# A transformer block on one core: merged narrow diagonal steps, a ring of five exponentials, a written-out order, and the maxima's splitting on GpSimd

## What is computed

```
x = x + 0.5 * ffn(layernorm(x), W_gate, W_qkv)      # layer 0
x = x + attn(layernorm(x), gamma, beta, W_in, ...)  # the branch: gates, a scan over time, W_out, W_skip
x = x + 0.5 * ffn(layernorm(x), W_gate, W_qkv)      # layer 1
```

```
gating = softmax(x @ W_gate.T); pick the top head h of each row
q, k, v = split(x @ W_qkv.T);  k_shared = k[h];  v_shared = v[h] * gating[h]
att = softmax(causal(q_head @ k_shared.T / 4));  y_head = att @ v_shared
```

## Time and profile before

| | |
|---|---|
| median of three runs | 886.76 us |
| span of the profiled execution, which is its own time | 889.9 us |
| busy: TensorE, VectorE, ScalarE, GpSimd | 844.8, 747.1, 720.6, 295.7 us |
| mean granted TensorE clock | 0.974 of full speed |
| exponentials on ScalarE | 802, mean 767 ns |
| masks on GpSimd | 256, mean 411 ns |

### The profile page before, as it was taken

One profiled execution on the slowest core, in us unless ns is written; L12 is line 12 of the kernel. 1 busy time (PEld: TensorE's weight loads), 2 busy tenths in 40 slices (PEclk: granted clock), 3 DMA queues, 4 the chain that ended last, 5 costly groups with the idle time before them and its releaser, 6 DMA issues.

```text
span 889.9 us, 19042 instructions
## 1 busy us (share of the span) xinstructions
PE 844.8 (95%) x6460; PEld 291.6 (33%) x6460; DVE 747.1 (84%) x2379; ACT 720.6 (81%) x1169; POOL 295.7 (33%) x568
## 2 busy tenths in 40 slices
PE   9898999999999999999999999999999999999997
PEld 6433423332222332324233433342223323222221
DVE  5898778999999989887945889999998999999920
ACT  1148677868998788888979887889998788999996
POOL 3225404633104415046355445632113424110110
PEclk9899689999999999999999999999999999999999
DMA  6110000110000000100010002000001000000000
GB/s 189 49 43 19 2 2 5 57 43 20 1 2 2 1 1 1 43 18 3 1 53 9 2 2 61 3 1 26 1 1 39 25 25 3 24 3 1 2 1 24
DMA packets 20256, 18.03 MB, mean 20 GB/s; under 512 B 4144, under 2 KB 20160, under 8 KB 20160
## 3 DMA queue, kind: packets, MB, share of 16 engines
q1 hardware_dynamic: 19072, 15.74, 5.8%
q10 hardware_dynamic: 1088, 1.07, 0.4%
HBM read 10.24 MB, written 6.29 MB: 19 GB/s over the span
## 4 chain that ended last, share of the span: by engine, by line
PE 59%; DVE 18%; issue 9%; ACT 9%; POOL 5%; DMA 0%; POOLq 0%; SPq 0%; ACTq 0%; DVEq 0%
PE ps L1758 20%; PE ps L1724 12%; PE ps L1746 11%; DVE ps L1448 7%; DVE mxp L1445 5%; ACT probs L1229 5%; PE ps L1642 3%; ACT relu L1217 2%; PE ps L1690 2%; DVE mxp L1448 2%; PE ps L1657 2%; PE ps L1647 2%; PE ps L1565 1%; POOL u L937 1%; POOL u_x L986 1%
## 5 line engine op out<-in xcount | busy, mean ns | idle before, releaser
L1229 ACT ACTIVATE probs<-ps 128x1024 f32<-128x1024 f32 (+5 forms) x802 | 554.9, 767 | 81.2 <-PE ps L1746 76.3
L1758 PE MATMUL ps<-probs,v_l 128*32 128x512 f32 (+3 forms) x2560 | 301.9, 549 | 2.9 <-DVE mxp L1445 0.6
L1448 DVE CUSTOM_DVE_ANT_0 ps<-ps,mask 128x384 f32<-128x384 f32 (+3 forms) x512 | 234.2, 524 | 28.7 <-PE ps L1724 26.7
L1746 PE MATMUL ps<-q_t,k_tl 50*128 50x512 f16 (+3 forms) x1280 | 240.0, 356 | 14.4 <-ACT probs L1229 3.9
L1445 DVE TENSOR_REDUCE mxp<-ps 128x1 f32<-128x512 f32 x384 | 240.2, 683 | 12.7 <-PE ps L1724 10.1
L1724 PE MATMUL ps<-k_tl,q_t 48*128 48x512 f16 (+3 forms) x1152 | 239.4, 340 | 6.9 <-ACT k_tl L1127 1.9
L971 POOL TENSOR_SCALAR_AFFINE_SELECT probs<-probs 128x256 f32<-128x256 f32 x256 | 102.1, 411 | 396.4 <-ACT probs L1229 394.6
L1448 DVE CUSTOM_DVE_ANT_0 ps<-ps,relu 128x256 f32<-128x256 f32 (+1 forms) x256 | 136.1, 586 | 16.3 <-PE ps L1724 15.4
L1724 PEld LDWEIGHTS ps<-k_tl,q_t 48*128 48x128 f16 x1152 | 74.8, 95 | 158.9 <-DVE mxp L1445 48.1
L1746 PEld LDWEIGHTS ps<-q_t,k_tl 50*128 50x128 f16 x1280 | 65.6, 94 | 182.3 <-ACT probs L1229 85.3
L1217 ACT ACTIVATE relu<-ps 128x512 f32<-128x512 f32 x192 | 106.8, 621 | 5.7 <-PE ps L1724 5.2
(11 more groups left out here) (182 smaller groups left out, 633.2 us busy)
## 6 DMA issues: line engine op xcount, KB each, us to landing
q_t<-q_scratch SPq DMA_DIRECT2D x96, 64.0 KB, 2.2
q_scratch<-q_part SPq DMA_DIRECT2D x16, 256.0 KB, 2.2
out_dram<-x_sb SPq DMA_DIRECT2D x4, 512.0 KB, 2.9
x_sb<-in_L_attn_x_dram SPq DMA_DIRECT2D x3, 512.0 KB, 5.1
q_t<-m_row SPq DMA_DIRECT2D x64, 4.0 KB
wqkv_n<-in_L_ffn_W_qkv_dram ACTq DMA_DIRECT2D x1, 768.0 KB, 5.5
w_in_sb<-in_L_attn_W_in_dram SPq DMA_DIRECT2D x1, 384.0 KB, 5.5
x_sb<-in_L_attn_x_dram ACTq DMA_DIRECT2D x1, 256.0 KB, 3.5
```

The source lines that it names most:

```text
L1229: last = a_.activation(out if len(banks) == 1 else out[:, n:n + 1, :], bank[:, :, P * i:QW], ACT.Exp, scale=SCALE / LIFT ** 2)
L1448: last = v_.tensor_tensor_reduce(scores, scores, added, 1.0, LOWEST, ALU.add, ALU.max, accum_out=to)
L1746: last = mm(ps[:, BANK[e][n], P * i:QW], k_cols(ROWS_XM, hh, l, kt, P), q_rows(ROWS_XM, c, g, hh, P * i, QW - P * i), start=True, stop=True)
L1758: last = mm(out_bank[VW * hh:VW * hh + VW, P * i:QW], v_l[:, l, kt, :], probs[:, s % NB, hh, P * i:QW], start=j == 0, stop=j == key_tiles( ...
```

## The change

Four things change.

Steps of 256 and 128 columns (`NARROW`) have one score item for all four heads in place of two. Two heads share a bank, side by side: heads 0 and 2 in the first bank, 1 and 3 in the second. One exponential and one mask then take the four heads. The counts that the waits use follow (`EXPS`, `MASKS`).

The ring `probs` has five steps.

The splitting of the maxima goes to GpSimd, as three instructions: the scaled maxima in fp32, the same rounded to fp16, and their difference. VectorE keeps the reduction ahead of them. Its wait for the last transposition is now GpSimd's, and VectorE waits for GpSimd's last split of the unit before.

The order of all after the first chunk's preparation is written out: `PICKS` has one character an item, a digit for the list it is taken from (0 scores, 1 sums, 2 maxima and joins, 3 ends, 4 rows, 5 side work), or a letter for a filler item of so many matmuls. The timekeeper still chooses the banks. Its search, its look ahead and the due steps go.

```diff
-NB = 4
-LAG = 3
+NB = 5
...
-PER_STEP = 2
+NARROW = QW // 2
...
-    "join": (0, [("DVE", 750)]), "row": (100, [("ACT", 230)]),
+    "join": (0, [("DVE", 290), ("POOL", 1000)]), "row": (100, [("ACT", 230)]),
...
-TURN_MODE, ROW_TRIP, QUERY_TRIP = 110, 2300, 6000
+TURN_MODE, ROW_TRIP, QUERY_TRIP = 97, 2300, 6000
...
+def per_step(s):
+
+    return 1 if width(s) <= NARROW else 2
...
+PICKS = (
+    "55222222222225522252555422225522205255520050240222052200552122202212201115220312420225511002112200235422222022",
...
+    lists = [iter(work) for work in (scores, sums, maxima, ends, rows, SIDE)]
+    for pick in "".join(PICKS):
+        if pick.isalpha():
+            order.append(("warm", warm, ord(pick) - ord("a") + 1, min(clock.free) <= clock.at["PE"]))
             warm += 1
-            continue
...
+        else:
+            order.append(next(lists[int(pick)]))
+        clock.place(order[-1])
     return order, clock.bank
...
+EXPS = list(accumulate(per_step(s) for s in range(len(STEPS))))
+MASKS = list(accumulate(per_step(s) * DIAGONAL[s] for s in range(len(STEPS))))
...
+        mxs = sb("mxs", [P, GH * TC])
...
                         pool.wait_ge(s_exp, exp_no(s, k))
-                        pr = probs[:, s % NB, 2 * k:2 * k + 2, P * j:P * j + P]
+                        n = GH // per_step(s)
+                        pr = probs[:, s % NB, n * k:n * k + n, P * j:P * j + P]
                         g_.affine_select(out=pr, in_=pr, compare_op=ALU.is_ge, fill=0.0, base=0,
-                                         pattern=[[0, 2], [1, P]], channel_multiplier=-1).then_inc(s_msk, 1)
+                                         pattern=[[0, n], [1, P]], channel_multiplier=-1).then_inc(s_msk, 1)
...
+            def join(e):
+
+                v = e[1]
+                pool.wait_ge(s_c1, v + 1)
+                if v:
+
+                    pool.wait_ge(s_fill, filled(("row", v - 1)))
+                g_.tensor_scalar(mxs[:, :], mxf[:, :], 1.0 / M_SCALE, None, ALU.mult)
+                g_.tensor_scalar(mx2_p[:, :, 0, :], mxf_p, 1.0 / M_SCALE, None, ALU.mult).then_inc(s_c2, 1)
+                pool.wait_ge(s_c2, v + 1)
+                g_.tensor_tensor(mx2_p[:, :, 1, :], mxs[:, :].rearrange("p (o x) -> p o x", o=2), mx2_p[:, :, 0, :],
+                                 op=ALU.subtract).then_inc(s_mx, 1)
...
-                    out = probs[:, s % NB, 2 * k:2 * k + 2, P * i:QW]
-                    banks = scores_of(s, k)
-                    for n, bank in enumerate(banks):
-                        last = a_.activation(out if len(banks) == 1 else out[:, n:n + 1, :], bank[:, :, P * i:QW],
-                                             ACT.Exp, scale=SCALE / LIFT ** 2)
+                    w = width(s)
+                    n = GH // per_step(s) // 2
+                    out = probs[:, s % NB, 2 * n * k:2 * n * k + 2 * n, P * i:QW].rearrange("p (x o) q -> p o x q", o=2)
+                    done = 0
+                    for both in scores_of(s, k):
+                        scores = ps[:, both, QW - n * w:QW].rearrange("p o (x q) -> p o x q", x=n)
+                        banks = both.stop - both.start
+                        last = a_.activation(out[:, done:done + banks], scores, ACT.Exp, scale=SCALE / LIFT ** 2)
+                        done += banks
                     last.then_inc(s_exp, 1)
...
                     if v:

-                        dve.wait_ge(s_fill, filled(("row", v - 1)))
+                        dve.wait_ge(s_mx, v)
                     slots = mxp[:, :, :, :, 0:c + 1].rearrange("p o h i s -> p o (h i) s")
                     v_.tensor_reduce(mxf_p, slots, axis=AX, op=ALU.max).then_inc(s_c1, 1)
                     dve.wait_ge(s_c1, v + 1)
-                    v_.tensor_scalar(mx2_p[:, :, 0, :], mxf_p, 1.0 / M_SCALE, None, ALU.mult).then_inc(s_c2, 1)
-                    dve.wait_ge(s_c2, v + 1)
-                    v_.scalar_tensor_tensor(mx2_p[:, :, 1, :], mxf_p, 1.0 / M_SCALE, mx2_p[:, :, 0, :],
-                                            ALU.mult, ALU.subtract).then_inc(s_mx, 1)
-                    dve.wait_ge(s_mx, v + 1)
...
-                    for n in range(2):
-                        hh = 2 * e[2] + n
-                        last = mm(ps[:, BANK[e][n], P * i:QW], k_cols(ROWS_XM, hh, l, kt, P),
+                    heads, w = GH // per_step(s), width(s)
+                    for n in range(heads):
+                        hh, col = heads * e[2] + n, QW - (heads // 2 - n // 2) * w
+                        last = mm(ps[:, BANK[e][n % 2], col:col + w], k_cols(ROWS_XM, hh, l, kt, P),
                                   q_rows(ROWS_XM, c, g, hh, P * i, QW - P * i), start=True, stop=True)
                     last.then_inc(s_qk, 1)
```

More of the change, by code:

```diff
@@ L3 @@
 from contextlib import ExitStack
+from itertools import accumulate
 T = 2048
@@ L158 @@
 SPLIT = [("scale", n) for n in range(2)] + [("split", n) for n in range(5)]
[L159 to L164, removed]
+SIDE = prepare(0, 1) + [("bias",), ("size",)] + SPLIT + prepare(0, 2) + prepare(0, 3) + branch(0) + prepare(1, 0) \
+    + branch(1) + prepare(1, 1) + branch(2) + prepare(1, 2) + branch(3) + prepare(1, 3)
 RINGED = {"weights", "scale", "wgate", "range", "bias", "turn", "gate", "kv", "q", "keys", "gates", "skip", "rec", "fin", "row", "max",
@@ L202, in width @@
     return QW - P * key_tile(UNITS[u][1], j)[1]
+def per_step(s):
+    return 1 if width(s) <= NARROW else 2
 def weights(e, past):
     if e[0] == "qk":
-        mask = [("POOL", 460)] if STEPS[e[1]][1] < TC else []
-        return 0.44 * width(e[1]), "rows", [("ACT", EXP + EXP_COLUMN * width(e[1]) * 2)] + mask
+        heads = GH // per_step(e[1])
+        mask = [("POOL", 230 * heads)] if STEPS[e[1]][1] < TC else []
+        return 0.22 * heads * width(e[1]), "rows", [("ACT", EXP + EXP_COLUMN * width(e[1]) * heads)] + mask
     if e[0] == "pv":
@@ L229, in weights @@
     pe, then = WEIGHT[e[0]]
-    return pe, "full", then
+    return pe, "columns" if e[0] == "row" else "full", then
 def unit_no(l, c, g):
@@ L271, in __init__ @@
         self.mode = self.past = None
-        self.summing = False
         self.stretch, self.streamed, self.full = FIRST_W - 1.0, 0.0, True
[L274 to L294, removed]
     def run(self, t, work):
@@ L342, in ready @@
             u, j = STEPS[e[1]]
-            if ("qk", e[1], 1) not in ended:
+            scores = ("qk", e[1], per_step(e[1]) - 1)
+            if scores not in ended:
                 return None
-            t = max(t, ended["qk", e[1], 1] + TO_PE)
+            t = max(t, ended[scores] + TO_PE)
             return max(t, min(self.free)) if j == 0 else t
@@ L432, in place @@
                     self.free[b] = t + TO_PE
-            self.done[engine] += took
             reach = TO_NEXT
-        if e[0] in ("pv", "oev"):
-            self.summing = e[0] == "pv" and e[1] not in LAST
         if e[0] == "oev":
@@ L461, in weave @@
         order.append(e)
-    scores = [("qk", s, hp) for s in range(len(STEPS)) for hp in range(2)]
+    scores = [("qk", s, hp) for s in range(len(STEPS)) for hp in range(per_step(s))]
     sums, maxima, ends, rows = [], [], [], []
@@ L472, in weave @@
         rows.append(("row", u))
[L473 to L483, removed]
-                continue
[L485 to L537, removed]
-            warm += 1
[L539 to L543, removed]
+    lists = [iter(work) for work in (scores, sums, maxima, ends, rows, SIDE)]
@@ L583 @@
 DIAGONAL = [j < TC for _, j in STEPS]
-DIAGONAL_BEFORE = [sum(DIAGONAL[:s]) for s in range(len(STEPS))]
+EXPS = list(accumulate(per_step(s) for s in range(len(STEPS))))
+MASKS = list(accumulate(per_step(s) * DIAGONAL[s] for s in range(len(STEPS))))
 TURNED, _last = {}, None
@@ L601, in exp_no @@
 def exp_no(s, k):
-    return PER_STEP * s + k + 1
+    return EXPS[s] - per_step(s) + k + 1
 def filled(e):
@@ L839, in scores_done @@
         def scores_done(u):
-            return exp_no(LAST[u], PER_STEP - 1)
+            return EXPS[LAST[u]]
         @block.sync
@@ L978, in attention @@
                                      op=ALU.add).then_inc(s_xa, 1)
+            mx2_p = mx2[:, :].rearrange("p (o a x) -> p o a x", o=2, a=2)
+            mxf_p = mxf[:, :].rearrange("p (o x) -> p o x", o=2)
+            def join(e):
[8 more added lines that the diff above has]
+                                 op=ALU.subtract).then_inc(s_mx, 1)
             def halve(e):
@@ L1085, in _ @@
                     attention(e)
+                elif e[0] == "join":
+                    join(e)
                 elif e[0] == "stats":
@@ L1749, in attention @@
                 else:
-                    pe.wait_ge(s_exp, exp_no(s, PER_STEP - 1))
+                    pe.wait_ge(s_exp, EXPS[s])
                     if DIAGONAL[s]:
-                        pe.wait_ge(s_msk, PER_STEP * (DIAGONAL_BEFORE[s] + 1))
+                        pe.wait_ge(s_msk, MASKS[s])
                     if j == 0:
```

29 lines of the change are left out of this document (23 added, 6 removed).

## The result

The changed kernel takes 846.3 us (four runs, 842.2 to 846.6); its ratio to the kernel before is 0.950, interval 0.9465 to 0.9536. I had forecast 872 and a range down to 856. The profiled execution has a span of 844.3 us, 45.6 less than before.

The account below looks back on a forecast made before the run. TensorE, VectorE and ScalarE, all nearly full, were taken to bound the kernel in turn. 2.9 + 9.5 + 2.8 + 1.1 - 1.5 = 14.8 us off 889.9 gave 875.1, scaled to 872 us; range 856 to 886.

Parts of the forecast that it names:

- my signs of being wrong: Listed observations that would refute the forecast; the one meant is ScalarE's exponentials in more split pieces than 162.
- GpSimd's three: The three 128x16 splitting instructions GpSimd gains per unit: between 0.6 and 1.35 us, taken as 0.85, 27 us in all.
- Masks of double size: GpSimd's 64 merged masks on narrow diagonal steps: between 411 and 822 ns each, costing nothing that counts.
- The wait for split maxima: TensorE waiting at the row's transposition for the splitting, 0.5 us later on GpSimd: mostly covered, charged 3 x 0.5 = 1.5 us.
- D: Rival: with half the fillers gone, another half-clock stretch like 96 to 120 us costs 12 us, hence 884 us; chance 0.07.
- The order: TensorE's written-out list: 29 fewer changes of kind give 2.9 us, 44 fewer fillers 9.5 (bounds 0 and 14).
- the sum as a sum: Adding separately priced terms for order, VectorE, ScalarE and the splitting's delay: 14.8 us saved, 872 us after scaling.
- Exponentials merged: 64 fewer exponentials on narrow diagonal steps, 188 or 182 ns each: 11.8 us off ScalarE, 1.1 counted by chain share.
- the 7 us that I allowed for the banks: Exponentials split where banks aren't neighbours: new banks may change their number by a third, 7 us either way; taken as zero.
- The splitting moved: Splitting of maxima to GpSimd: 15.8 us off VectorE, 2.8 counted by chain share, against 1.5 charged for delay.
- rival C: The join on GpSimd becomes the path, queued behind late masks, so the kernel is slower: 896 us; chance 0.07.
- Rival A: The new order avoids TensorE's early wait and the half-clock stretch after it, up to 12 us more: 860 us; chance 0.22.

Follow-up runs that it names:

- new_fewer_splits: The changed kernel with its choice of banks taking two neighbouring banks if free up to 0.6 us later than the two earliest: 858.7 us, ratio 0.967.
- new_two_exps: The changed kernel with its narrow steps' exponentials always in two instructions, one a bank; merged TensorE items, masks, banks and order stay: 845.2 us, ratio 0.949.
- my own lists: Orders by a search keeping 400 partial orders; with all three parts 878.3 us, with the splitting left on VectorE 861.9 us.
- my widest search: Ring of five and merged narrow steps, splitting still on VectorE, order by a search keeping 400 partial orders: 861.9 us, ratio 0.968 to the kernel before.

## Why the prediction was wrong

**The direction and several sizes held.** VectorE: 15.8 us forecast with its idle time, 14.9 of busy time measured. ScalarE: 11.8 forecast for 64 exponentials, 8.2 measured, but with the price found below the nearness is luck. Split exponentials were 187 for 162, one of my signs of being wrong. GpSimd's three: 0.85 us a unit forecast, 0.72 measured. Masks of double size: 635 ns, inside 411 to 822. The wait for split maxima: 1.5 us charged, 0.4 found. Past 130 us the clock was at 0.50 for 3.4 us near 276 us, where the kernel before had three such spells; a stretch of the size in D didn't come.

**The step that failed is "The order", and with it the sum as a sum.** I priced the order by what it shows by itself, 29 changes of kind and 44 fillers, 12.4 us, and the parts by their shares of the chain, 3.9. The runs show that neither exists alone: this order without the two parts 0.998, the parts without the order 1.018, both 0.950. The gain is an interaction, which a sum of prices taken one by one has no term for. In the sum's own terms: the fillers fell by 14.8 us where I had 9.5, at the top of my bounds, while TensorE's visible idle time, which I had at no change, fell from 45.1 to 31.2 us, and its other records by 17, for which I had the 2.9 of the changes of kind. Without the fillers of its list the new order still runs at 848 us.

**"Exponentials merged" had the wrong price, and most likely the wrong engine.** I took differences of single durations, 188 and 182 ns, for what an instruction more costs. They overlap: with the order kept, 39 more cost ScalarE 2.2 us and 149 fewer saved 7.9, 0.05 to 0.06 us each. The same price is in my 11.8 us and in the 7 us that I allowed for the banks. In the new order the merge took 4.1 us off ScalarE's busy time and 33 us off the kernel's. With 8 us less of exponentials the changed kernel got slower (new_fewer_splits), and with 39 more instructions no slower (new_two_exps). I had the right resource in one sentence, "holds two PSUM banks where it held four", and gave it no price. That the banks are what the merge pays with is my reading, not shown: TensorE's waits for them fit it (10.7 us without the merge, 2.2 with), but no run let a merged item hold four banks, and its one mask for two and its fewer items weren't tested by themselves.

**"The splitting moved" held only in its place.** In the new order it gains 10 us against my 2.8; in the old one it loses 13, by the wait that rival C named, 12.6 us; in my own lists the kernel with it is 16 us slower, not by rival C's wait. The rule of GPSIMD Engine Reference, Engine selection, in the Trainium skill (elementwise work belongs on VectorE) would have it slower; the measurements decide by the order, and at 128x16 the two engines' instructions are close, 251 and 218 ns here against 218 and 205 before.

**Rival A** came true in part. Fillers behind the gap alone give 7 us of the 12 I allowed. In the changed kernel the stop is shorter and the stretch falls from 24 to 10 us; over the whole kernel the lost clock falls from 23.1 us (0.026 of 889.9) to 12.7, by the ratios above some 6 to 8 of the 45.6 us. So rival A is a smaller part of the gain, and its 860 us missed for the same reason as the forecast.

**What stays open.** How much of the changed kernel's lead over my widest search (846 against 862) is the quality of its list, and how much chance in how it meets the clock. Nor is it known what in the new order the merge needs. I found no version that is faster than the changed kernel beyond the noise (new_two_exps, 845.2 for 846.3).

## What to carry to other kernels

When a kernel's engines run in fixed queues and three of them are nearly full, price a change of parts and a change of order together or not at all: a part dropped into an order made for other durations can cost what it was meant to save, and a good order for other parts is an ordinary one. Test the table of both by both before you argue shares. In such a kernel look at TensorE's waits for banks and at its clock as well as at another engine's busy time. Take the price of an instruction more from a run that keeps the order, not from the difference of two durations.

## What the runs showed of the hardware

A single stop of TensorE of 1.7 us stood ahead of 24 us at the 1.2 GHz level. With seven filler matmuls there, behind a stop of 1.34 us, it stayed at 2.4 GHz, which gave 7.3 us of 890; in the changed kernel a stop of 0.67 us stood ahead of 10 us at 1.2 GHz. Two exponentials of 128x512 in a row took 1.08 us, one of 128x1024 took 1.02, so the second instruction cost 0.06 us although each is 614 ns long by itself. On GpSimd an instruction on a 128x16 tile takes 218 to 254 ns, near VectorE's 205 to 218, and its mask of 128x512 takes 635 ns where one of 128x256 takes 415.
